# The products that make keys and queries: one of 128 weight columns, or two of 64 side by side

## Chip, cores and metric

One core of a Trainium2 chip runs the kernel. The metric is the device time of one execution in microseconds (us). Engines are written as in the profile: PE is TensorE's matmuls, PEld its weight loads (both are issued by one sequencer, in program order), DVE is VectorE, ACT is ScalarE, POOL is GpSimd, SP is SyncE, which only issues DMAs here.

## What is computed

A transformer block in float32 on 4 batches of 1024 tokens of width 128: a layer norm and attention with 16 heads of width 64 and rotary positions, then a layer norm and a feed-forward net of width 352 whose inputs and weights are rounded to blockwise FP4.

```python
qkv = xn @ w_qkv                                # (4,1024,128) @ (128,3072)
q, k, v = to_heads(...)                         # 16 heads of 64
qr, kr = rotate(q), rotate(k)
scores = jnp.einsum('bhid,bhjd->bhij', qr, kr) * scale
probs = jax.nn.softmax(scores, axis=-1)
out = jnp.einsum('bhij,bhjd->bhid', probs, v)
x = x + (out @ w_out + b_out)
x = x + _L0_ffn_ref(_layernorm(x, axis=-1), w_gate, w_up, w_down)
```

## The kernel before

**Pairs and slots.** The attention runs over 32 pairs P = 0 to 31 (two heads of 64, so 128 partitions; 8 pairs for each batch), with two rounds of lead-in (P = -2 and -1) and one behind. Each engine walks the pairs with an order written out by hand. A pair has 8 slots, d = 0 to 7, and in each slot PE does, in this order: a unit of maxima (`max_scores`, L1212: scores of high parts alone, from which the softmax takes its row maxima), two steps of `scores` (L1156, into `st`), a second unit of maxima, at most one K, V or O unit, two steps of `times_v` (L1169: probabilities times values, into `po`), and at last at most one B or S unit (or, in a few pairs, X or Y).

**Units.** All K, V, O, B, S, X and Y units write one PSUM bank, `ms`, in one fixed order. Each waits until the bank was read out (`ms_free`). The slots hold:

```python
UNITS = (
    (("K", 0),), (("K", 1), ("S", 1)), (("K", 2), ("B", 1)), (("K", 3),),
    (("V", 0),), (("V", 1), ("S", 0)), (("O", 0), ("B", 0)), (("O", 1),))
```

The four K units of a pair (`project_kq`, L1182 to L1194) make keys (u = 0, 1) and queries (u = 2, 3) of the pair P + 2, 512 tokens each. Each is one float32 product of 128 rows by 128 weight columns by 512 tokens. In the trace a float32 product is two MATMULs (two passes), each with its LDWEIGHTS. In pairs 0 to 29 each K unit stands between a unit of maxima and the two steps of `times_v`. In the lead-in the four units of pair 0 follow each other and go to four different banks, and those of pair 1 stand between units of maxima. There are 128 K units, 120 of them in pairs 0 to 29. Pairs 30 and 31 have none.

**Tilings of the PE array.** Maxima and scores use two tiles of 64 rows by 128 columns, one for each head. `times_v` uses two tiles of 128 rows by 64 columns, a head in each: the two products of a step write partitions 0 to 63 and 64 to 127 of `po`. The sums of the softmax (S, L1229) use four tiles of 128 by 32. K, V, O and transposes use the whole array, 128 by 128.

**Readers.** DVE reads a K unit in `rope_parts`: times cosine (L919), times sine (L920, which frees `ms`). In every slot DVE reduces both units of maxima (L893 for two halves at once, L895 and L897 when ACT copies one half first, L687), each in its turn. In slots 1, 3, 5 and 6 it also adds the probabilities of the first two key tiles (`first_keys`, L909), in slots 3 and 7 it takes reciprocals of sums (L939), in slot 2 it gathers the column of maxima (L902). Each unit of maxima waits until DVE has reduced the one before it in the same bank (`mx_free`). The B unit (L1220) transposes the maxima for ACT's `spread_maxima` (L674). ACT does the exponentials (L659) and the copies of `po` (L698), and POOL adds the probabilities of the other key tiles (L398) and does most of the rotary adds.

**Special pairs.** Pairs 5, 13 and 21 carry the transposes of the next batch (X units in slots 3 and 4) and its normalisation on ACT; pairs 11, 19 and 27 the normalisation of a finished batch on ACT. After the pairs comes the feed-forward net, which has no K unit.

Of the kernel before, what the change touches and what calls it, by code (L numbers as in the profile page):

```python
# [17 lines left out]
HEADS, HD = 16, 64  # L18
# [10 lines left out]
CH = 512  # L29
# [31 lines left out]
def block_program(nc, ctx, x_d, gamma_d, beta_d, wqkv_d, wout_d, bout_d, wg_d, wu_d, wd_d,  # L61
                  cos_d, sin_d, ident_d, sums_d, recips_d, out_d):
    def sb(name, shape, dt=F32):
        return ctx.enter_context(nc.sbuf_tensor(name, shape, dt))

    def sem(name):
        return ctx.enter_context(nc.semaphore(name))
# [12 lines left out]
    wqkv = sb("wqkv", [PART, 2, 3, PART])  # L80
# [78 lines left out]
    mx_full, mx_free, ms_full, ms_free = (sem(n) for n in ("mx_full", "mx_free", "ms_full", "ms_free"))  # L159
# [75 lines left out]
    def unit_bank(L, u):  # L235

        return (ms, po, mx[:, 0], mx[:, 1])[u] if L == 0 else ms
# [9 lines left out]
    def read_out(engine, unit):  # L247

        engine.wait_ge(ms_free, order_of[unit] + 1)
# [859 lines left out]
    def _(pe):  # L1109
        mm = nc.tensor.matmul  # L1110
# [3 lines left out]
        for c in range(2):  # L1114
            pe.wait_ge(xn_done, HALF * c + HALF)
            for t in range(HALF):
                last = nc.tensor.transpose(halves[c][:, bass.ts(t, PART)], xn[:, HALF * c + t, :], ident[:, :])
# [15 lines left out]
        def bank(unit):  # L1133

            wait(pe, ms_free, order_of[unit])
# [37 lines left out]
        def batch(X):  # L1173
            return xnT[:, (X // PPB) * TOKENS:(X // PPB + 1) * TOKENS]
# [9 lines left out]
        def project_kq(L, u):  # L1184
            s, c = u // 2, u % 2
            if L > 0:
                bank(("K", L, u))
            if u == 0:
                pe.wait_ge(xnT_done, 2)
                if L // PPB > 0:  # L1190
                    read_out(pe, ("X", L // PPB, 1))
            pe.wait_ge(pair_in[L % 2], 16 * (L // 2 + 1))
            mm(unit_bank(L, u)[:, :], wqkv[:, L % 2, 1 - s, :], batch(L)[:, bass.ts(c, CH)], start=True, stop=True)\  # L1193
                .then_inc(ms_full, 1)  # L1194

        def max_scores(N, u):
            banks, t, half = max_unit(N, u)
# [44 lines left out]
        def pair(P):  # L1242
            for d in range(JT):
# [9 lines left out]
                for kind, X, u in units_at(P, d):  # L1253
                    if kind == "K":
                        project_kq(X, u)
                    if kind == "V":
                        project_v(X, u)
                    if kind == "O" and present(P):
                        output_projection(X, u)
# [129 lines left out]
```

## Time and profile before

| what | value |
|---|---|
| median of 3 runs | 1579.3 us (1578.39 to 1579.79) |
| the profiled execution, its own time | 1578.3 us |
| its span | 1576.5 us |
| PE matmuls, share of the span busy | 95% |
| POOL | 85% |
| DVE | 74% |
| ACT | 57% |
| mean granted TensorE clock | 0.982 |

The profile shows one execution. The span is the time from the first to the last profiled instruction, 1.8 us less than that execution's time. A busy share is a mean over stages with different limits, and a busy PE includes the time that a product sits in the array before its data streams.

### The profile page before, as it was taken

The page shows a single profiled execution, that of the slowest core. Times are in us where ns is not written, and L with a number is a line of the kernel's source. Part 1 is how long each engine was busy: PE and PEld are TensorE (multiplying, and loading weights), DVE is VectorE, ACT ScalarE, POOL GpSimd, SP SyncE. Part 2 cuts the span into 40 slices and gives each one's busy share as a digit, 9 for nine tenths or more (in the row PEclk, how much of TensorE's full clock was granted, in tenths as well). Part 3 has the DMA queues.
Part 4 walks back from the last instruction along what each step waited for, and adds up shares of the span by engine and source line. Part 5 has one row for each costly group of instructions (what it writes and reads, how often), then busy time and mean ns, then how long its engine had stood idle before and what let it go on. Part 6 is the DMA issues. An engine that isn't in the chain of part 4 may idle for free.

```text
span 1576.5 us, 25643 instructions
## 1 busy us (share of the span) xinstructions
PE 1501.7 (95%) x9257; PEld 786.5 (50%) x9257; DVE 1162.1 (74%) x1566; ACT 896.3 (57%) x1384; POOL 1345.7 (85%) x789
## 2 busy tenths in 40 slices
PE   4899999999999999999999999999999999998677
PEld 2345555555455455555545455555554455554455
DVE  7787776777777777777777777777777777764787
ACT  1366556666556666665655666666565656663222
POOL 3699999789889899998889899999889899975774
PEclk8799999999999999999999999999999999999789
DMA  5212111111111111111111111111121111100001
GB/s 139 54 28 49 38 45 48 40 48 48 49 40 32 48 40 43 49 40 48 48 47 43 30 48 35 48 48 40 48 48 44 36 40 48 30 17 23 7 15 34
DMA packets 69197, 67.10 MB, mean 43 GB/s; under 512 B 26512, under 2 KB 52432, under 8 KB 69072
## 3 DMA queue, kind: packets, MB, share of 16 engines
q1 hardware_dynamic: 69072, 65.46, 16.5%
q8 instruction: 75, 1.23, 0.3%
q14 instruction: 50, 0.41, 0.1%
HBM read 29.25 MB, written 2.62 MB: 20 GB/s over the span
## 4 chain that ended last, share of the span: by engine, by line
PE 89%; DVE 7%; issue 2%; ACT 1%; DMA 0%; SPq 0%; ACTq 0%; DVEq 0%
PE po L1169 30%; PE st L1156 24%; PE mx L1212 11%; PE ms L1193 8%; PE ms L1180 4%; PE ms L1238 4%; PE ms L1229 4%; PE ms L1220 1%; PE mx L1297 1%; PE st L1297 1%; DVE probs L848 1%; DVE st L842 1%; DVE negmax L893 1%; DVE probs L1061 0%; ACT xnT L637 0%
## 5 line engine op out<-in xcount | busy, mean ns | idle before, releaser
L398 POOL TENSOR_TENSOR psum_keys<-psum_keys,probs 128x1024 f32<-128x1024 f32 x256 | 609.0, 2379 | 94.6 <-ACT probs L659 73.9
L659 ACT ACTIVATE probs<-st 128x1024 f32<-128x1024 f32 x512 | 497.4, 1028 | 134.3 <-PE st L1156 129.9
L1169 PE MATMUL po<-probs,v 128*64 128x512 f32 x2048 | 495.9, 605 | 0.0
L893 DVE TENSOR_REDUCE negmax<-mx 128x2 f32<-128x1024 f32 x322 | 393.3, 1222 | 129.4 <-PE mx L1212 129.2
L895 DVE TENSOR_REDUCE negmax<-mx 128x1 f32<-128x512 f32 x186 | 128.6, 692 | 212.4 <-PE mx L1212 212.4
L1169 PEld LDWEIGHTS po<-probs,v 128*64 128x64 f32 x2048 | 124.2, 136 | 256.2 <-issue 171.5
L1212 PE MATMUL mx<-keys_hi,queries_hi 64*128 64x512 f32 x1016 | 229.5, 448 | 11.9 <-ACT max_copy L687 5.3
L1156 PE MATMUL st<-queries_hi,keys_lo 64*128 64x512 f32 x1024 | 202.4, 392 | 0.0
L1156 PE MATMUL st<-queries_lo,keys_hi 64*128 64x512 f32 x1024 | 202.0, 391 | 0.0
L1156 PE MATMUL st<-queries_hi,keys_hi 64*128 64x512 f32 x1024 | 201.2, 389 | 0.0
L1212 PEld LDWEIGHTS mx<-keys_hi,queries_hi 64*128 64x128 f32 x1016 | 96.0, 185 | 160.3 <-issue 123.9
L398 POOL TENSOR_TENSOR psum_keys<-probs 128x1024 f32<-128x1024 f32 x64 | 152.5, 2383 | 25.1 <-ACT probs L659 25.1
L674 ACT ACTIVATE max_rows<-ms,mask 128x128 fp32r<-128x128 f32 x256 | 79.4, 369 | 148.8 <-PE ms L1220 148.8
L909 DVE TENSOR_REDUCE first_sum<-probs 128x512 f32<-128x1024 f32 x128 | 158.6, 1239 | 6.0 <-ACT probs L659 6.0
L531 POOL TENSOR_TENSOR kq<-kq 128x1024 f32<-128x1024 f32 x62 | 147.8, 2383 | 17.1 <-DMA kq<-sin_part 16.6
L1193 PE MATMUL ms<-xnT,wqkv 128*128 128x512 f32 x250 | 145.1, 663 | 1.3 <-ACT xnT L606 0.9
L897 DVE TENSOR_REDUCE negmax<-max_copy 128x1 f32<-128x512 f32 x186 | 127.7, 687 | 9.6 <-ACT max_copy L687 9.4
L687 ACT ACTIVATE max_copy<-mx 128x512 f32<-128x512 f32 x186 | 111.0, 597 | 12.8 <-PE mx L1212 0.4
L1156 PEld LDWEIGHTS st<-queries_hi,keys_hi 64*128 64x128 f32 x1024 | 96.4, 185 | 22.3
L1156 PEld LDWEIGHTS st<-queries_lo,keys_hi 64*128 64x128 f32 x1024 | 96.2, 184 | 22.5
L1156 PEld LDWEIGHTS st<-queries_hi,keys_lo 64*128 64x128 f32 x1024 | 96.8, 186 | 14.4 <-issue 2.0
L682 ACT ACTIVATE sums_kept<-ms 128x256 f32<-128x256 f32 x64 | 24.6, 384 | 132.0 <-PE ms L1229 132.0
(173 smaller groups left out, 1808.2 us busy)
## 6 DMA issues: line engine op xcount, KB each, us to landing
kq<-sin_part SPq DMA_DIRECT2D x256, 128.0 KB, 2.4
rsum<-recips SPq DMA_DIRECT2D x128, 128.0 KB, 2.9
wqkv<-in_L_attn_w_qkv_dram SPq DMA_DIRECT2D x32, 192.0 KB, 2.8
resid<-in_L_attn_x_dram SPq DMA_DIRECT2D x4, 512.0 KB, 8.3
wout<-in_L_attn_w_out_dram SPq DMA_DIRECT2D x32, 64.0 KB, 2.5
out_dram<-resid SPq DMA_DIRECT2D x8, 256.0 KB, 2.3
sums<-sums_kept SPq DMA_DIRECT2D x64, 4.0 KB
spread<-sums SPq DMA_DIRECT2D x64, 4.0 KB, 1.5
```

The lines of the kernel that those rows point to most:

```text
L398: nc.gpsimd.tensor_tensor(psum_keys[:, c], first, probs[:, (STEPS * P + i) % RING], ALU.add)\
L531: add = nc.gpsimd.tensor_tensor(raw[s], raw[s], swp[s], ALU.add)
L659: nc.scalar.activation(probs[:, step_n % RING], st[step_n % 2][:, :], ACT.Exp, scale=SCALE)\
L687: nc.scalar.activation(max_copy[:, :], mx[:, 1], ACT.Copy).then_inc(max_copied, 1)
L893: nc.vector.tensor_reduce(out, banks[:, :], AX.X, ALU.max, negate=True).then_inc(mx_free, 1)
L895: nc.vector.tensor_reduce(out[:, 0:1], banks[:, 0], AX.X, ALU.max, negate=True).then_inc(mx_free, 1)
L897: nc.vector.tensor_reduce(out[:, 1:2], max_copy[:, :], AX.X, ALU.max, negate=True).then_inc(copy_reduced, 1)
L909: nc.vector.tensor_reduce(first_sum[:, c, a], probs[:, 0:FIRST_KEYS, a].rearrange("p r n -> p n r"), AX.X, ALU.add).then_inc(key_part, 1)
L1156: last = mm(st[step_n % 2][:, a], stationary[rows], moving[rows], start=(n == 0 and tile < 2), stop=(n == len(terms) - 1), skip_group_chec ...
L1169: last = mm(po[HD * a:HD * a + HD, :], v[:, P % 2, KEY_ORDER[jt], HD * a:HD * a + HD], probs[:, step_n % RING, a], start=(jt == 0), stop=( ...
L1193: mm(unit_bank(L, u)[:, :], wqkv[:, L % 2, 1 - s, :], batch(L)[:, bass.ts(c, CH)], start=True, stop=True)\
L1212: last = mm(banks[:, a, :], queries_hi[rows, N % SETS, bass.ts(t, PART)], keys_hi[rows, N % SETS, keys], start=(half == 0), stop=True, ski ...
```

## The change

`project_kq` issues two products where it issued one. The first takes weight columns 0 to 63 and writes partitions 0 to 63 of the bank, the second takes columns 64 to 127 and writes partitions 64 to 127. Both stream the same 512 columns of `xnT`. The semaphore is raised by the second. This is the form that `times_v` has. Nothing else changes: the same numbers, the same order of units, the same waits.

```diff
             pe.wait_ge(pair_in[L % 2], 16 * (L // 2 + 1))
-            mm(unit_bank(L, u)[:, :], wqkv[:, L % 2, 1 - s, :], batch(L)[:, bass.ts(c, CH)], start=True, stop=True)\
-                .then_inc(ms_full, 1)
+            for a in range(2):
+                cols = slice(HD * a, HD * a + HD)
+                last = mm(unit_bank(L, u)[cols, :], wqkv[:, L % 2, 1 - s, cols], batch(L)[:, bass.ts(c, CH)],
+                          start=True, stop=True)
+            last.then_inc(ms_full, 1)
```

## Rows read from the trace of the kernel before

**Rows 1.** The page: busy time by engine, and the chain's share by line.
```profile
PE 1501.7 (95%) x9257; PEld 786.5 (50%) x9257; DVE 1162.1 (74%) x1566; ACT 896.3 (57%) x1384; POOL 1345.7 (85%) x789
...
PE po L1169 30%; PE st L1156 24%; PE mx L1212 11%; PE ms L1193 8%; PE ms L1180 4%; PE ms L1238 4%; PE ms L1229 4%; PE ms L1220 1%; PE mx L1297 1%; PE st L1297 1%; DVE probs L848 1%; DVE st L842 1%; DVE negmax L893 1%; DVE probs L1061 0%; ACT xnT L637 0%
```

**Rows 2.** Timeline, PE, pair 9, slot 1: start, duration, line, form, count.
```profile
451.14 0.39 PE L1212 MATMUL mx<-keys_hi,queries_hi 64*128 64x512 f32 x2
451.45 0.70 PE L1193 MATMUL ms<-xnT,wqkv 128*128 128x512 f32 x1
451.99 0.59 PE L1193 MATMUL ms<-xnT,wqkv 128*128 128x512 f32 x1
452.51 0.65 PE L1169 MATMUL po<-probs,v 128*64 128x512 f32 x2
452.99 1.03 PE L1169 MATMUL po<-probs,v 128*64 128x512 f32 x4
...
453.85 0.60 PE L1169 MATMUL po<-probs,v 128*64 128x512 f32 x2
454.38 0.42 PE L1229 MATMUL ms<-first_sum,ones 128*32 128x256 f32 x4
```

**Rows 3.** Timeline, weight loads of the same slot.
```profile
451.45 0.19 PEld L1193 LDWEIGHTS ms<-xnT,wqkv 128*128 128x128 f32 x1 [0.35 <-issue]
452.51 0.20 PEld L1169 LDWEIGHTS po<-probs,v 128*64 128x64 f32 x4 [0.76 <-ACT probs L659]
```

**Rows 4.** Timeline, PE, pair 30, slot 0, which has no K unit.
```profile
1367.06 0.39 PE L1212 MATMUL mx<-keys_hi,queries_hi 64*128 64x512 f32 x2
1367.38 0.65 PE L1169 MATMUL po<-probs,v 128*64 128x512 f32 x2
```

**Rows 5.** The line of the K units: count, shortest, median and longest pass.
```profile
L1193 PE MATMUL ms<-xnT,wqkv x250: 592/697/1222, 17.6 to 1340.1; 128*128 128x512 f32 x125
```

**Rows 6.** Timeline, DVE, pair 9: slot 1, and the start of slot 2.
```profile
453.31 0.68 DVE L920 TENSOR_TENSOR sin_part<-ms,sin 128x512 f32<-128x512 f32 x1
455.92 0.69 DVE L895 TENSOR_REDUCE negmax<-mx 128x1 f32<-128x512 f32 x1 [0.78 <-PE mx L1212]
```

**Rows 7.** Timeline, pair 9, slot 2: the reader of K 2, then B 1.
```profile
459.51 0.68 DVE L920 TENSOR_TENSOR sin_part<-ms,sin 128x512 f32<-128x512 f32 x1
460.34 0.14 PEld L1220 LDWEIGHTS ms<-ident,maxcol 128*128 128x128 f32 x1 [0.81 <-DVE sin_part L920]
```

**Rows 8.** Timeline, lead-in: a V unit that waits for DVE.
```profile
25.07 0.68 DVE L920 TENSOR_TENSOR sin_part<-mx,sin 128x512 f32<-128x512 f32 x1
25.80 0.19 PEld L1180 LDWEIGHTS ms<-wqkv,xnT 128*128 128x128 f32 x1 [3.56 <-DVE sin_part L920]
```

**Rows 9.** Timeline, pair 9, slots 3 and 4: DVE, then the second maxima of slot 4.
```profile
462.75 1.23 DVE L893 TENSOR_REDUCE negmax<-mx 128x2 f32<-128x1024 f32 x1 [0.23 <-PE mx L1212]
465.08 1.24 DVE L909 TENSOR_REDUCE first_sum<-probs 128x512 f32<-128x1024 f32 x1
466.35 1.17 DVE L893 TENSOR_REDUCE negmax<-mx 128x2 f32<-128x1024 f32 x1
467.58 0.19 PEld L1212 LDWEIGHTS mx<-keys_hi,queries_hi 64*128 64x128 f32 x2
```

**Rows 10.** Timeline, DVE, pair 5, slot 4: the same reduction there.
```profile
292.29 1.23 DVE L893 TENSOR_REDUCE negmax<-mx 128x2 f32<-128x1024 f32 x1 [0.26 <-PE mx L1212]
```

**Rows 11.** Timeline, pair 0: DVE in slots 0 and 1, then the second maxima.
```profile
59.19 1.22 DVE L893 TENSOR_REDUCE negmax<-mx 128x2 f32<-128x1024 f32 x1
60.45 0.19 PEld L1212 LDWEIGHTS mx<-keys_hi,queries_hi 64*128 64x128 f32 x2 [0.87 <-DVE negmax L893]
```

**Rows 12.** Timeline, ACT: what starts its long run in pairs 5 and 11.
```profile
273.87 0.60 ACT L698 ACTIVATE oT<-po 128x512 f32<-128x512 f32 x1 [2.12 <-PE po L1169]
542.28 0.38 ACT L682 ACTIVATE sums_kept<-ms 128x256 f32<-128x256 f32 x1 [2.92 <-PE ms L1229]
```

**Rows 13.** Busy time in the stretch of pair 12: window, length, engines, PEclk.
```profile
575.40:618.70 43.30, 43.30 (x276) 22.19 (x274) 32.76 (x42) 26.09 (x38) 41.94 (x24) 1.00 0.17 44
```

## Prediction

> **What bounds the kernel.** I read the page first. PE is busy 95% of the span, and the chain that ended last is almost all PE: lines L1169, L1156, L1212 and L1193 alone make up 73% of it [rows 1]. So in the pairs PE's own program sets the time, and whatever shortens PE's work by a true amount shortens the span, unless PE then meets a wait. POOL is busy 85% and DVE 74%, and neither is in the chain for long. The second view is the timeline of one slot of an undisturbed pair, of PE and of its weight loads [rows 2, 3]; the third is the timeline of DVE around each K unit, where I look for what PE meets when it comes earlier [rows 6 to 11].
>
> **What a K unit costs now.** The line's view counts 250 passes into `ms`, two for each of 125 units, with a median duration of 697 ns [rows 5]; but the reader should look at starts, not durations, since a MATMUL's duration includes its time in the array. The unit starts at 451.45, its second pass at 451.99, the first product of `times_v` at 452.51: 1.06 us in all [rows 2]. Then the passes of `times_v` start at 452.51, 452.99 and on to 453.85, which is 0.48 us and twice 0.43 us, two products side by side in each (a wave) [rows 2]. So a wave of 512 columns streams in 0.43 us, and the unit's two waves are 0.86 us. The other 0.20 us of 1.06 are two things. The first pass can't stream until its 128 columns are loaded: 0.54 - 0.43 = 0.11 us. After its last wave `times_v` starts 0.52 us later, not 0.43: 0.09 us between tilings. `times_v` then pays for its own first load of 64 columns: 0.48 - 0.43 = 0.05 us.
>
> **The change, part by part.**
>
> *Before the unit.* A change of tiling from the maxima to the unit stays. Maxima to K take 451.45 - 451.14 = 0.31 us [rows 2], and maxima to `times_v`, in pair 30 where no K unit stands between, 1367.38 - 1367.06 = 0.32 us [rows 4]. So the switch into the 64-column tiling costs what the switch into the whole array costs: 0.
>
> *The unit.* It becomes two products, four MATMULs, four loads. In `times_v` two such products cost two waves, not four, and the four loads at its start are over in 0.20 us, the later ones under the first wave [rows 3]. The nearest rows for the new unit are these, with the same form. So the unit is 0.05 us of first load and two waves of 0.43 us.
>
> *Behind the unit.* `times_v` follows in the same tiling. Its first load can go under the unit's last wave, as between its own two steps, where the spacing is 0.43 us [rows 2].
>
> The sum from unit start to the second wave of `times_v`: now 1.06 + 0.48 = 1.54 us, then 0.48 + 0.43 + 0.43 = 1.34 us. That is 0.20 us less. The bounds: if only the unit's own first load is halved, 0.05 us; it can't be over 0.21 us, since two waves remain. I take 0.20, as `times_v` shows all three terms in the same form. One thing no row shows: both products stream the same columns of `xnT`, while those of `times_v` stream different ones. That is a rival below.
>
> 120 units by 0.20 us would be 24 us. How much is kept depends on what PE meets, slot by slot.
>
> *Slot 0 (K 0) and slot 1 (K 1).* Behind K 1 and `times_v` stands S 1, which needs the bank read out. DVE ends L920 at 453.31 + 0.68 = 453.99, S 1 starts at 454.38 [rows 2, 6]. It would start at 454.18, still 0.19 behind. What a true wait needs is shown in the lead-in: L920 ends at 25.75, the waiting PE starts at 25.80, 0.05 us [rows 8]. So nothing is met. DVE's next reduction has 0.78 us of idle time before it [rows 6]. Both slots keep 0.20 us. In pair 0 they keep nothing: DVE there goes straight from the maxima of slot 0 over K 0's two reads to the reduction at 59.19, which ends at 60.41, and PE's maxima start 0.04 us later, at 60.45, after a wait [rows 11]; slot 1 is alike. In pairs 5, 13, 21 and 11, 19, 27 PE waits over 1 us for ACT in the slot that follows, but ACT's run is started by PE's `times_v` or S unit, behind the K unit [rows 12], so the gain moves through. 58 units by 0.20 = 11.6 us.
>
> *Slot 2 (K 2).* Behind it stands B 1. L920 ends at 459.51 + 0.68 = 460.19, B 1 starts at 460.34, 0.15 us later [rows 7]; in 30 pairs it is 0.15 or 0.16. A wait needs 0.05, so B 1 can come 0.10 us earlier and no more. DVE is not sped up by the change: it goes from the maxima over L902 and L919 to L920 without a pause. The other 0.10 us is a new wait. 30 by 0.10 = 3.0 us.
>
> *Slot 3 (K 3).* From 462.75 on DVE has no idle time: maxima, cosine, sine, L909, L939 and the maxima of slot 4, which end at 466.35 + 1.17 = 467.52. PE's second maxima of slot 4 start at 467.58, 0.06 us later, which is the delay of a true wait [rows 8, 9]. This DVE run was released by maxima ahead of K 3 and doesn't wait for K 3. So PE is already late here by DVE, and a shorter K 3 gains 0; PE only waits longer. It is so in 27 of 30 pairs. In pairs 5, 13 and 21 an X unit makes PE's slot longer, and DVE idles 0.26 us [rows 10]: these three keep 0.20, so 0.6 us.
>
> *POOL.* The pair with least room is pair 12: POOL is busy 41.94 of 43.30 us at a granted clock of 1.00 [rows 13]. A pair would shrink by 0.20 + 0.20 + 0.10 = 0.50 us to 42.8, still above.
>
> *The lead-in.* The units of pair 0 end while DVE still works for others, those of pair 1 mostly wait for DVE; I count 0.
>
> Sum: 11.6 + 3.0 + 0.6 = 15.2 us. The profiled execution's 1578.3 becomes 1563.1 (span 1561.3). It lies 1.0 us under the median, so against the median of 1579.3 the forecast is 1564.1. With unit savings between 0.15 and 0.21 us the range of this case is 1563 to 1568.
>
> **The rivals.**
>
> *All is kept.* DVE's runs shift with PE after all and 120 units gain 0.20: 24 us, 1555.3. Against it stand the delays of 0.06 us in slot 4 [rows 9]. 0.06.
>
> *The array still pauses between K and `times_v`*, say because the bank changes. Only half of the first load is saved: 91 units (58 + 30 + 3) by 0.05 = 4.6 us, 1574.7. Against it: S's waves follow `times_v` with changed tiling only, and the two steps of `times_v` change weights and data without pause [rows 2]. 0.07.
>
> *Loads don't hide under products.* Then the second pass and the first wave of `times_v` each wait 0.05 us for their 64 columns. The saving is 0.20 - 0.10 = 0.10 us, by 91 units = 9.1 us: 1570.2. Against it: the later loads of the step lie under its first wave, and no further wave is longer than 0.43 us [rows 2, 3]. 0.04. The Trainium skill speaks for this one ("TensorE: Matmul & The Clock Gate", Part 3): a weight load overlaps a running product only where the two use different row groups, and here both tiles use all rows. The trace doesn't agree so far, as `times_v` is in the same case and streams at 0.43 us a wave.
>
> *Another wait eats the gain in slots 0 and 1*, on DVE or ACT, half of 11.6 us: about 9.4 us kept, 1570. Against it: 0.78 us idle on DVE [rows 6]. 0.07.
>
> *Slower: the two products go one behind the other*, because they stream the same columns of `xnT` at once. Its place is each K unit: four waves, not two, 0.86 us more and 0.20 saved, 0.66 us lost by 118 units (pair 0's first two are hidden) = 78 us, 1657. It decides from the point at which more than 0.20 of the second product's 0.86 us is not side by side with the first. For it: no row has two tiles with the same moving data. Against it: all other tilings here overlap, two by two and four by four [rows 2]. 0.05.
>
> **Numbers.** The forecast has 0.70. About 0.2% (3.2 us) is what a measurement of this kernel can tell from no change. The range 1557 to 1571.5 holds the forecast, the third and the fourth case, 0.81, and some of the first's neighbourhood. Faster by over 0.2%: 0.91 (all but the slow case and the part of the second that lies too near). Within: 0.04. Slower: 0.05.
>
> **What would show it.** In the changed trace, slot 1: K starts, waves at +0.48 and +0.91, `times_v` right there with waves 0.43 apart from its first. Pairs shrink from 43.3 to 42.8 us. B 1 starts 0.05 us behind L920's end with PE idle before it. PE's wait for DVE ahead of slot 4's second maxima grows by 0.20 us. K passes begin in twos, not one by one. Wrong would be: a gap between K and `times_v`, K waves in fours, slot 4 unchanged in its delay, or pairs at 42.5.

## The result and the profile after

The changed kernel takes 1562.7 us in the median of 4 runs (1562.61 to 1563.08), the kernel before 1578.91 (1578.39 to 1579.79, 4 runs). The ratio is 0.990, 95% interval 0.988 to 0.991: 16.2 us less. The forecast was 15.2 us less. The profiled execution's span went from 1576.5 to 1560.9 us, 15.6 less.

The page of the changed kernel, busy time by engine. It answers to [rows 1]: PE is busy 16.7 us less with 256 MATMULs more, the other engines do the same work.

```profile
PE 1485.0 (95%) x9513; PEld 784.8 (50%) x9513; DVE 1162.2 (74%) x1566; ACT 897.0 (57%) x1384; POOL 1346.8 (86%) x789
```

Timeline of PE in pair 9, slot 1, as in [rows 2] (the K unit is L1195 now, maxima L1215):

```profile
447.00 0.39 PE L1215 MATMUL mx<-keys_hi,queries_hi 64*128 64x512 f32 x2
447.31 0.65 PE L1195 MATMUL ms<-xnT,wqkv 128*64 128x512 f32 x2
447.80 0.60 PE L1195 MATMUL ms<-xnT,wqkv 128*64 128x512 f32 x2
448.22 0.60 PE L1169 MATMUL po<-probs,v 128*64 128x512 f32 x2
...
449.08 0.60 PE L1169 MATMUL po<-probs,v 128*64 128x512 f32 x2
449.51 0.60 PE L1169 MATMUL po<-probs,v 128*64 128x512 f32 x2
450.04 0.42 PE L1232 MATMUL ms<-first_sum,ones 128*32 128x256 f32 x4
```

The passes come in twos. Unit start, second wave at +0.49, `times_v` at +0.91, and from there 0.43 a wave with no longer first step. From the unit's start to the second wave of `times_v` it is 0.91 + 0.43 = 1.34 us, where it was 1.54. To S it is 450.04 - 447.31 = 2.73 us, where it was 454.38 - 451.45 = 2.93.

Weight loads of the same unit, as in [rows 3]:

```profile
447.31 0.20 PEld L1195 LDWEIGHTS ms<-xnT,wqkv 128*64 128x64 f32 x4 [0.36 <-issue]
```

All four loads are over in 0.20 us, the last two under the unit's first wave.

Slot 2, timeline of DVE and the load of B 1 (L1223 now), as in [rows 7]:

```profile
455.18 0.68 DVE L920 TENSOR_TENSOR sin_part<-ms,sin 128x512 f32<-128x512 f32 x1
455.92 0.14 PEld L1223 LDWEIGHTS ms<-ident,maxcol 128*128 128x128 f32 x1 [0.91 <-DVE sin_part L920]
```

L920 ends at 455.86 and B 1 starts 0.06 us later, the delay of a true wait (0.05 in [rows 8]); before it was 0.15.

Slots 3 and 4, DVE and the second maxima of slot 4, as in [rows 9]:

```profile
458.33 1.23 DVE L893 TENSOR_REDUCE negmax<-mx 128x2 f32<-128x1024 f32 x1 [0.23 <-PE mx L1215]
...
460.66 1.25 DVE L909 TENSOR_REDUCE first_sum<-probs 128x512 f32<-128x1024 f32 x1
461.82 0.20 DVE L939 RECIPROCAL spread<-spread 128x8 f32<-128x8 f32 x1
461.94 1.18 DVE L893 TENSOR_REDUCE negmax<-mx 128x2 f32<-128x1024 f32 x1
463.17 0.19 PEld L1215 LDWEIGHTS mx<-keys_hi,queries_hi 64*128 64x128 f32 x2 [0.31 <-DVE negmax L893]
```

From the start of DVE's run to the load of the maxima that wait for it: 463.17 - 458.33 = 4.84 us, and before 467.58 - 462.75 = 4.83. So most of K 3's 0.20 us is gone in that stretch.

What waits there is the weight load, and the wave of the maxima is another matter. PE before, and then after:

```profile
467.50 0.40 PE L1156 MATMUL st<-max_rows,one_rows 64*128 64x512 f32 x2
467.74 0.40 PE L1212 MATMUL mx<-keys_hi,queries_hi 64*128 64x512 f32 x2
```

```profile
462.89 0.40 PE L1156 MATMUL st<-max_rows,one_rows 64*128 64x512 f32 x2
463.17 0.50 PE L1215 MATMUL mx<-keys_hi,queries_hi 64*128 64x512 f32 x2
463.60 0.38 PE L1180 MATMUL ms<-wqkv,xnT 128*128 128x128 f32 x1
```

Before, the maxima start 0.24 us behind the last score wave, as score waves follow each other (0.23): their load was late, but still soon enough, and no wave waited. After, load and maxima start together at 463.17, and the wave still needs its columns, 0.11 us by the prediction's own number. The V unit behind shows the same: it starts 0.43 us after the maxima, and 0.33 before (468.07 - 467.74). That is 0.28 + 0.11 = 0.39 us behind the last score wave instead of 0.24, the 0.15 us that slot 4 loses in the table below. By the same number the load of before, at 467.58, would have let the wave go at 467.69, and it went at 467.74: some 0.05 us of room, worked out from these rows.

**Where the time went.** I took from the PE timeline the start of the first score step of each slot and subtracted. Sums over pairs 1 to 29, and one plain pair (9), changed less before, in us:

| slot | 0 | 1 | 2 | 3 | 4 | 5 to 7 |
|---|---|---|---|---|---|---|
| pair 9 | -0.21 | -0.19 | -0.08 | -0.20 | +0.15 | 0.00 |
| pairs 1 to 29 | -5.7 | -5.7 | -2.7 | -5.7 | +4.0 | 0.0 |

Pair 9 went from 43.33 to 42.80. From the start of pair 1 to that of pair 31 it is 15.8 us less. Pair 0 is 0.5 longer, the stretch from the start of pair 31 on is 0.2 shorter, and so is the one ahead of pair 0. Together that is the 15.6 us of the span, within rounding.

### The profile page after: what moved, and what is told of

It reads as the page before. It is cut to its first block, busy times and chain, and to the rows that moved or that the text cites. A ratio compares the mean times of both kernels' runs of the same rounds, so it can differ in the third digit from the quotient of the medians.

```text
span 1560.9 us, 26155 instructions
## 1 busy us (share of the span) xinstructions
PE 1485.0 (95%) x9513; PEld 784.8 (50%) x9513; DVE 1162.2 (74%) x1566; ACT 897.0 (57%) x1384; POOL 1346.8 (86%) x789
## 4 chain that ended last, share of the span: by engine, by line
PE 90%; DVE 7%; issue 2%; ACT 1%; DMA 0%; ACTq 0%; DVEq 0%
PE po L1169 29%; PE st L1156 24%; PE mx L1215 11%; PE ms L1195 8%; PE ms L1180 5%; PE ms L1241 4%; PE ms L1232 4%; PE ms L1223 1%; PE mx L1300 1%; PE st L1300 1%; DVE probs L848 1%; DVE st L842 1%; DVE negmax L893 1%; DVE probs L1061 0%; ACT xnT L637 0%
## 5 line engine op out<-in xcount | busy, mean ns | idle before, releaser
L1169 PE MATMUL po<-probs,v 128*64 128x512 f32 x2048 | 489.8, 599 | 0.0
L1169 PEld LDWEIGHTS po<-probs,v 128*64 128x64 f32 x2048 | 134.8, 136 | 233.9 <-issue 182.0
L1215 PE MATMUL mx<-keys_hi,queries_hi 64*128 64x512 f32 x1016 | 232.0, 453 | 12.6 <-DVE negmax L893 6.2
L1215 PEld LDWEIGHTS mx<-keys_hi,queries_hi 64*128 64x128 f32 x1016 | 95.9, 185 | 166.0 <-issue 124.8
L1195 PE MATMUL ms<-xnT,wqkv 128*64 128x512 f32 x500 | 138.4, 633 | 1.9 <-DVE sin_part L920 1.1
```

The costliest lines, as they stand in the source:

```text
L1169: last = mm(po[HD * a:HD * a + HD, :], v[:, P % 2, KEY_ORDER[jt], HD * a:HD * a + HD], probs[:, step_n % RING, a], start=(jt == 0), stop=( ...
L1195: last = mm(unit_bank(L, u)[cols, :], wqkv[:, L % 2, 1 - s, cols], batch(L)[:, bass.ts(c, CH)], start=True, stop=True)
L1215: last = mm(banks[:, a, :], queries_hi[rows, N % SETS, bass.ts(t, PART)], keys_hi[rows, N % SETS, keys], start=(half == 0), stop=True, ski ...
```

## The experiments

Each kernel was timed in turn with the kernel before on the same chip; differences are of medians. Part numbers and slot sums come from the profiled execution of each kernel, by the same subtraction as above.

### One K unit at a time

The theory: K 0 and K 1 keep 0.20 us each, K 2 keeps 0.10, K 3 almost nothing. The rival: all four give alike. The edit is the width of the products in `project_kq`, here for the first kernel (`HD` is 64):

```diff
-            for a in range(2):
-                cols = slice(HD * a, HD * a + HD)
+            width = PART if u == 3 else HD
+            for at in range(0, PART, width):
+                cols = slice(at, at + width)
```

K 3 whole again, the others in two products:

> K 3 alone goes back to one product of 128 columns; K 0, K 1 and K 2 stay as in the changed kernel (which took 16.2 us off). Theory: in 27 of 30 pairs DVE's unbroken run from slot 3 to slot 4 sets the time there, so K 3's 0.20 us were worth at most 0.05 us in those and 0.20 in pairs 5, 13 and 21: 27 x 0.05 + 3 x 0.20 = 1.9 us come back, 14.3 us less than before. Rival (each K unit gave the same share, and the total fell short for another reason): a quarter comes back, 12.2 us less than before.

Measured: 1564.73 against 1579.41, 14.7 us less; by the interval 12.0 to 16.6. In the trace slots 3 and 4 are as before.

K 3 alone in two products (`HD if u == 3 else PART`):

> Only K 3 is two products; K 0, K 1 and K 2 are whole. Theory: 1 to 2 us less than before, and PE waits about 0.2 us longer for DVE ahead of the second maxima of slot 4. Rival of equal shares: 4.0 us less than before.

Measured: 1578.14 against 1579.41, 1.3 us less; the ratio is 0.9996, interval 0.9987 to 1.0005, so it can't be told from no change, but 4.0 us less is outside it. In the trace, over pairs 0 to 29, slot 3 is 6.0 us shorter in sum and slot 4 4.1 us longer.

K 0 and K 1 alone (`HD if u < 2 else PART`):

> Only K 0 and K 1 are two products. Theory: 58 units keep 0.20 us each, 11.6 us less than before (up to 12.5 with small effects in the pairs where DVE or ACT is late). Rival of equal shares: half of 16.2, 8.1 us less than before.

Measured: 1567.14 against 1579.41, 12.3 us less. In the trace slot 1 gives 5.9 us in sum, slot 0 6.2.

K 2 whole again (`PART if u == 2 else HD`):

> K 2 alone goes back to one product; K 0, K 1 and K 3 stay in two. Theory: K 2 kept only 0.10 us in each of 30 pairs, as B 1 waits for the reader: 3.0 us come back, about 13 us less than before. Rival (K 2 was worth its full 0.20 us): 6 us come back, about 10 us less than before.

Measured: 1566.43 against 1578.95, 12.5 us less. In the trace slot 2 is as before (-0.08 became +0.01 us in pair 9).

The theory said 14.3, 1 to 2, 11.6 to 12.5 and 13 us less, and 14.7, 1.3, 12.3 and 12.5 were measured. Equal shares would be 12.2, 4.0, 8.1 and again 12.2. The second and third kernel rule them out by their times. The first leaves them just inside its interval, and the last can't tell 12.2 from 13; it speaks against its own rival, 10 us, if narrowly (10.1 to 14.7 by the interval). For these two the slot sums of the traces decide, over pairs 0 to 29 and against the changed kernel: with K 3 whole, slots 3 and 4 together are 1.9 us longer, and with K 2 whole slot 2 is 2.9 us longer, where a quarter would be 4.0 each.

### What the 0.20 us is made of

The edit: `width = 32` for all K units, so four tiles of 128 by 32. The loads are shorter, but `times_v` needs another tiling.

> Every K unit is four products of 32 columns, side by side in the tiling of the softmax sums and not in that of times_v. The first load is shorter still (32 columns), but the tiling changes between the unit and times_v. Theory (the gain is 0.05 us of first load, 0.09 us of tiling change and 0.05 us of times_v's own first load): the last two are gone and the first becomes 0.08 us, so 91 units x 0.08 = 7.3 us less than before, 7 to 8.5. Rival (the gain comes from small weight loads alone, whatever the next tiling): at least 16 us less than before. Rival (products that stream the same data in four tiles go one behind the other): slower than before by over 50 us.

Measured: 1571.82 against 1579.41, 7.6 us less (ratio 0.996, 0.994 to 0.997). Timeline of PE in pair 9, slot 1, of this kernel:

```profile
449.10 0.64 PE L1196 MATMUL ms<-xnT,wqkv 128*32 128x512 f32 x4
449.55 0.61 PE L1196 MATMUL ms<-xnT,wqkv 128*32 128x512 f32 x4
450.09 0.65 PE L1169 MATMUL po<-probs,v 128*64 128x512 f32 x2
```

The unit takes 450.09 - 449.10 = 0.99 us. The step behind its last wave is 0.54 us, where it is 0.42 with tiles of 64: the change of tiling is back, 0.1 us, and `times_v` pays its own first load again. The shorter load itself gave 0.05 to 0.06 us in each slot. So of the 0.20 us over two thirds (0.09 of pause and 0.05 of `times_v`'s first load) come from the tiling that the unit shares with its successor, and some 0.06 from the unit's own shorter first load. The expectation came close partly by luck: it counted 0.08 us in 91 units, and the trace has 0.06 us in nearly all 120, as K 3's share is small enough here for the room of 0.05 us that slot 4 has. The Trainium skill ("TensorEngine Tiling (Array Packing)", Tiling Modes) says that a change of the tiling mode drains the array; by this rule the pause comes with this kernel and not with the changed one, and both traces agree. That four tiles stream one operand side by side, as two do in the changed kernel, speaks against the slow rival.

### Making room on DVE

If DVE's run hides K 3's gain, then breaking the run must bring it out. First both small pieces were moved from slot 3 into slot 4, between its two maxima:

```diff
                     if present(N):
                         row_maxima(N, u)
+                        if d == 4 and not second and present(P):
+                            first_keys(P, 0, 1)
+                            if present(F):
+                                reciprocals(F, 1)
...
-                if present(P) and d in (1, 3, 5, 6):
+                if present(P) and (d in (1, 5, 6) or d == 3 and not present(P + 1)):
                     first_keys(P, d // HALF, int(d in (3, 6)))
-                if d == 3 and present(F) and present(P):
+                if d == 3 and present(F) and present(P) and not present(P + 1):
                     reciprocals(F, 1)
```

> The changed kernel, with DVE's first_keys and reciprocals of slot 3 moved behind the first maxima of slot 4. Theory: DVE's unbroken run is broken, the second maxima of slot 4 no longer wait, and K 3's 0.20 us are kept: 10.39 us for slots 3 and 4 become 10.16, 26 pairs x 0.23 = 6 us less than the changed kernel. Rival (PE's lateness in slot 4 comes from something else, such as ACT's exponentials, or the moved work delays them): no gain.

Measured: 1563.13 against 1578.63, 15.5 us less, so no gain over the changed kernel's 16.2. Its four runs lie far apart, 1561.63 to 1564.76, and the trace is of the fastest, whose span is 1.1 us shorter than the changed kernel's. By the total the rival wins, by the trace neither does: slot 4 is 3.9 us shorter in sum, as meant, but slot 2 of pairs 11, 19 and 27 is 0.56 to 0.76 us longer, slot 0 of pair 21 0.50, and the stretch from pair 31 on 0.8. What makes the other runs longer still, no trace shows. POOL's waits, from the view of waits of this kernel:

```profile
POOL kq L531 <- DMA kq<-sin_part: 36.1, 26, 8.1
POOL oT L524 <- DMA rsum<-recips: 28.1, 18, 11.8
```

and of the changed kernel (sum in us, times, longest):

```profile
POOL oT L524 <- DMA rsum<-recips: 16.4, 3, 11.8
POOL kq L531 <- DMA kq<-sin_part: 16.0, 3, 9.2
```

The reciprocals start a chain of DMAs that SP issues ahead of those for the second rotary half (`return_reciprocals`, then `swap_halves`). Later reciprocals make POOL wait for both, 32 us more in all.

The same move with K 3 whole:

> The same move on DVE, with K 3 as one product of 128 columns. Theory: with DVE out of the way K 3's form is worth its full 0.20 us in 29 or 30 pairs, so this is 5.8 us slower than the kernel with the move and K 3 in two products (where without the move the form was worth under 2). Rival: the difference stays under 2.5 us.

Measured: 1567.64 on the same chip, 4.5 us more than with K 3 in two products. Without the move the form of K 3 was worth about 1.5 us (16.2 against 14.7). It is short of the 5.8 that the theory gave, but beyond the rival's 2.5. The traces of the two kernels have 5.9 us in slot 3.

Then `first_keys` alone was moved and the reciprocals stayed in slot 3:

> The changed kernel with first_keys (L909) alone moved from slot 3 behind the first maxima of slot 4; the reciprocals (L939) stay in slot 3. Theory: what the earlier move lost came from the reciprocals, which start the DMAs on which POOL waits; with these in place POOL's waits for DMAs are back at some 32 us in all (64 us with the earlier move), pairs 11, 19 and 27 lose nothing in slot 2, and slot 4 keeps 26 x 0.15 = 3.9 us: 4 to 5 us less than the changed kernel. Rival (the loss came from first_keys itself, by exponentials that wait for its buffers): pairs 11, 19 and 27 again lose 0.5 us or more in slot 2 and the total is within 1 us of the changed kernel.

Measured: 1561.21 against 1578.95, 17.7 us less, 1.5 better than the changed kernel and not 4 to 5. DVE in slots 3 and 4 of pair 9:

```profile
459.22 0.68 DVE L920 TENSOR_TENSOR sin_part<-ms,sin 128x512 f32<-128x512 f32 x1
459.82 0.19 DVE L939 RECIPROCAL spread<-spread 128x8 f32<-128x8 f32 x1
460.64 1.23 DVE L893 TENSOR_REDUCE negmax<-mx 128x2 f32<-128x1024 f32 x1 [0.62 <-PE mx L1217]
461.78 1.24 DVE L909 TENSOR_REDUCE first_sum<-probs 128x512 f32<-128x1024 f32 x1
```

The run is broken: DVE idles 0.62 us ahead of the maxima. POOL's waits for DMAs are back at 31.3 us:

```profile
POOL oT L524 <- DMA rsum<-recips: 16.1, 3, 11.4
POOL kq L531 <- DMA kq<-sin_part: 15.2, 2, 8.1
```

and slot 2 of pairs 11, 19 and 27 loses nothing, so both of that theory's marks are met. Slot 4 gives the 3.9 us. What takes some 2.4 of them back lies elsewhere: slot 0 of pairs 3, 4, 11, 19 and 27 is 0.9 us longer in sum (the last section says why), and the stretch from pair 31 to the end some 1.5 us longer. That stretch in the changed kernel (the windows view: length, then busy time of PE, PEld, DVE, ACT and POOL, and granted clock):

```profile
1389.50:1560.90 171.40, 129.85 (x693) 83.39 (x689) 116.87 (x169) 55.71 (x135) 109.42 (x71) 0.90 0.07 20
```

and in this kernel:

```profile
1386.70:1559.60 172.90, 131.80 (x693) 84.97 (x689) 116.88 (x169) 55.91 (x135) 109.56 (x71) 0.88 0.07 20
```

The work is the same, and the granted clock 0.88 against 0.90. PE waits much in the feed-forward part (28.6 us for one line of DVE in the changed kernel), and the granted clock is 0.50 there several times in both kernels, which is 1.2 GHz: for 42 us in sum in this kernel and for 34 in the changed one. In the traces of this study the stretch takes 171.5 to 172.5 us where the low clock lasts 34 to 36 us, and 172.9 and 173.2 in the two with 42. So the clock goes with the longer stretch, but a spread of 1 us is there without it, and what part of the 1.5 us is the clock's is not shown.

And with K 3 whole:

> first_keys alone moved, K 3 as one product. Theory: K 3's form is worth its full 0.20 us in 29 pairs, so 5.8 us more than the same kernel with K 3 in two products (with first_keys in slot 3 it was under 2). Rival: the difference stays under 2.5 us.

Measured: 1565.36, 4.2 us more than with K 3 in two products. In the traces slot 3 gives 6.3 us in sum and slot 4 is unchanged, as the theory says, and slot 0 of pairs 3, 4, 11, 19 and 27 gives 1.1 back. So with DVE out of the way the full 0.20 us of K 3 reach the time of the slots. Of the 5.8 us that were expected in the total 4.2 are left.

### The same form for the V and O units

They too stand between maxima and `times_v` and use the whole array.

```diff
             for t in range(HALF):
-                last = mm(ms[:, bass.ts(t, PART)], batch(N)[:, bass.ts(HALF * u + t, PART)], wqkv[:, N % 2, 2, :],
-                          start=True, stop=True)
+                for a in range(2):
+                    rows = slice(HD * a, HD * a + HD)
+                    last = mm(ms[rows, bass.ts(t, PART)], batch(N)[:, bass.ts(2 * (HALF * u + t) + a, HD)],
+                              wqkv[:, N % 2, 2, :], start=True, stop=True)
```

`output_projection` is edited alike.

> The changed kernel, with the V and O units too as products of 64 weight columns side by side (each product of 128 columns becomes two). They also stand between maxima and times_v. Theory: each unit gives up to 0.20 us. Behind V 0, O 0 and O 1 the trace shows room; V 1 is followed by S 0, which starts 0.15 us after ACT has copied V 1, so 0.10 is kept. 31 pairs x (0.20 + 0.10 + 0.20 + 0.20) = 21.7 us, less 1 to 3 us where DVE is late into the next pair: 19 to 21 us less than the changed kernel, 1542 to 1544. Rival (the gain needs the long stream of 512 columns; products of 128 columns are bound by their weight loads or by the issue of twice as many instructions): no gain or slower than the changed kernel.

Measured: 1539.34 against 1578.63, 39.3 us less (ratio 0.975, 0.974 to 0.977), 23.1 better than the changed kernel, a little more than expected. Against the changed kernel slot 4 of pair 9 gives 0.22, slot 5 0.14 and slots 6 and 7 0.22 and 0.23 us, which is 0.80 in sum where 0.70 was expected. Products of 128 columns gain as those of 512 do, since it is the start and the end of the unit that is paid for.

With the first move on DVE:

> V and O units in two products and the move on DVE together. Theory: the gains add, 25 to 27 us less than the changed kernel, 1536 to 1538. Rival: POOL, busy 41.9 us in pairs 12, 20 and 28, becomes the bound there as pairs shrink to about 41.9 us, and 1 to 3 us are lost.

Measured: 1544.98 against 1578.63, 33.7 us less: 5.6 worse than without the move. Slot 2 of pairs 11, 19 and 27 is 0.8, 5.1 and 2.9 us longer. ACT in pair 19, slot 2, and the POOL instruction that it waited for:

```profile
872.94 1.26 ACT L637 ACTIVATE xnT<-resid,ln_columns 128x128 f32<-128x128 f32 x3 [2.44 <-POOL ln_columns L479]
```

```profile
872.67 0.24 POOL L479 TENSOR_SCALAR ln_columns<-ln_columns 128x8 f32<-128x8 f32 x1
```

This is the rival's cause in another place, pairs 11, 19 and 27 and not 12, 20 and 28. POOL comes late to the layer norm's small steps. Its waits for the two DMAs are 59.8 us in sum in this kernel and 31.6 with the V and O units alone; that it is these that make it late is argued and not shown. ACT's run starts late, and the copy of maxima behind it is what PE waits for, 3.34 us here.

With `first_keys` alone moved:

> V and O units in two products, and first_keys alone moved. Theory: 4 us less than with the V and O units alone (1539.3), about 1535. Rival: POOL has no more room, pairs 11, 19 and 27 lose in slot 2 as with the earlier move, and the total is 1539 or more.

Measured: 1537.29 (1536.41 to 1539.2) against 1578.95, 41.7 us less (ratio 0.973, 0.972 to 0.975). That is between the theory's 1535 and the rival's 1539, and the interval overlaps that of the V and O units alone, so these two can't be told apart; both beat the changed kernel by over 20 us. In the traces slot 2 of pairs 11, 19 and 27 loses nothing, which speaks against the rival. Slot 4 gives 3.2 us in sum, but slot 0 takes 2.5 back, 1.3 of them in pair 0, and no run shows why.

## Why the prediction was right, point by point

**The unit's own saving.** Foreseen as 0.20 us, and measured so. The spacing of the waves was foreseen as 0.48 and 0.43, and is 0.49 and 0.42. That two products which stream the same columns of `xnT` run side by side, the one thing that no row had shown, is seen in the twos of the timeline. The slow rival falls.

**Slots 0 and 1.** 11.6 us foreseen for 58 units; the sums over pairs 1 to 29 are 5.7 and 5.7, 11.4. Of pair 0, counted as nothing, slot 1 kept 0.19 us too, and slot 0 is from 0.4 us shorter to 0.9 longer than before in the kernels of this study, so nothing can be read there.

**Slot 2.** 3.0 us foreseen, 2.7 measured; the new wait of PE for L920 is there with 0.06 us of delay.

**Slot 3.** 0.6 us foreseen for three pairs, and 0 for the others. Slots 3 and 4 together gave 1.7. The step that was wrong is "PE is already late here by DVE, and a shorter K 3 gains 0": in 26 pairs it gained 0.04 us each on average, 1.1 us in sum. The reading took the start of the weight load, 0.06 us behind DVE, for a late PE. The waves had not waited: in all 27 pairs the maxima started 0.22 to 0.25 us behind the last score wave. So K 3's gain first used up the 0.05 us of room and was lost only beyond it. The kernel with four products of 32 columns bears this out, as its 0.05 us of K 3 are kept. K 3's form was worth 1.3 and 1.5 us by the two experiments on it, close to 0.6 + 1.1, though the first of these can't be told from nothing by its time alone.

**The sum.** 11.4 + 2.7 + 1.7 = 15.8 us in the pairs' own stretch against 15.2. The medians differ by 16.2. The 0.4 us between are within what runs differ by, and nothing here settles them. The range that the prediction gave for this very case, 1563 to 1568, just misses the median of 1562.7, since its low end had nothing for K 3 in 27 pairs; the wide range, 1557 to 1571.5, holds it. The chances of the six cases add up to 0.99, which leaves 0.01 without a case.

**The rivals.** "All is kept" (24 us) falls by slots 2 and 4. "The array still pauses" (4.6 us) and "loads don't hide under products" (9.1 us) fall by the waves. The latter was the rule of the Trainium skill, "TensorE: Matmul & The Clock Gate", Part 3 (What overlaps and what doesn't), that loads overlap running products only in other row groups; the same part (The mechanism) also lets a load go ahead when it targets the background weight buffer, which would fit the rows. Here loads of both tiles, which use all rows, lie under a wave, and the next wave starts 0.42 us after the one before. Where page and measurement differ the measurement decides. "Another wait eats the gain in slots 0 and 1" falls by the sums. POOL, busy 86% now, didn't bind, but the experiments show how near it is: 32 us more of its waits for DMAs went with the loss of a gain of 4.

## What to carry to other kernels

Between blocks of products with different tilings of the array there was a pause, here 0.09 us, plus the first load of each block. A small unit that stands between blocks may take its successor's tiling by being split in halves side by side; here that cost nothing in streaming. What of it is kept is read slot by slot: follow each reader of the unit to the next instruction of the bounding engine that waits for it, and subtract the delay of a true wait from the slack. Look at the start of the wave and not only at that of its weight load: a load can wait while the array is still busy. And before moving work off a full engine, look at what the moved instructions start elsewhere.

## What was not expected of the hardware

A tiny DVE instruction can last as long as a POOL instruction beside it. In the kernel before, pair 3, slot 7, DVE and POOL:

```profile
223.66 2.29 DVE L1019 TENSOR_SCALAR ln_columns<-ln_columns 128x24 int32<-128x24 int32 x1
```

```profile
223.53 2.38 POOL L398 TENSOR_TENSOR psum_keys<-psum_keys,probs 128x1024 f32<-128x1024 f32 x1
```

The DVE instruction has 24 elements in each partition and ends at 225.95, 0.04 us after POOL's at 225.91. The view of its line gives 172 ns for the shortest of its six and 2291 for the longest. It makes DVE late into slot 0 of the next pair. The same line in the changed kernel, and in the one with `first_keys` alone moved:

```profile
L1019 DVE TENSOR_SCALAR ln_columns<-ln_columns x6: 120/2094/2178, 179.7 to 1458.7; 128x8 int32<-128x8 int32 x4, 128x24 int32<-128x24 int32 x2
L1021 DVE TENSOR_SCALAR ln_columns<-ln_columns x6: 172/2240/2326, 179.0 to 1455.7; 128x8 int32<-128x8 int32 x4, 128x24 int32<-128x24 int32 x2
```

Five of the six stand in slot 7 of pairs 2, 3, 10, 18 and 26, ahead of the slots 0 that move from kernel to kernel. How long one lasts depends on where in POOL's instruction it falls, and the traces show what that does, in the kernels whose V and O units are whole. Where it lasts 1.8 us or less, the slot 0 behind it has its plain length. With 1.99 us (kernel before, pair 10) slot 0 is 0.12 us over that, with 2.18 (changed, pair 3) 0.29, with 2.33 (`first_keys` moved, pair 3) 0.46. That is the 0.9 us above: with `first_keys` moved the five last 2.19 to 2.33 us, and in the changed kernel 2.09 to 2.18 and one, started as POOL ended, 0.12. No run changed this instruction by itself. The Trainium skill ("Trainium Architecture — The Big Picture", What this means for kernel authors) says that VectorE and GpSimd share a pair of ports to SBUF under an exclusive lock; by this rule the one waits out the other, as these rows show it.
